# Per-engine order tables, bank holds and expert roundings of a fused attention and mixture-of-experts kernel

## The reference

```python
x = L0_attn_x                       # (16, 512, 128)
xn = _layernorm(x, axis=-1)
x = x + attn(xn) + ffn(xn)

# attn: rmsnorm, 16 heads of 64
h = _rmsnorm(x, norm_scale)
q, k, v = (einsum('bsd,dhe->bshe', h, w) for w in (wq, wk, wv))
weights = softmax(einsum('bqhd,bkhd->bhqk', q * 64 ** -0.5, k))
out = einsum('bqhe,hed->bqd', einsum('bhqk,bkhd->bqhd', weights, v), w_out) + b_out

# ffn: a router (128 -> 512 -> 8) picks two of 8 experts (128 -> 512 -> 128) a token
logits = silu(x @ rw1 + rb1) @ rw2 + rb2
k_logits, k_index = top_k(logits, 2); k_prob = softmax(k_logits)
for e in range(8):
    we = sum(where(k_index == e, k_prob, 0))
    out = out + we[:, None] * (silu(x @ w1[e] + b1[e]) @ w2[e] + b2[e])
```

## Time and profile before

| | |
|---|---|
| median of three runs | 2102.24 us |
| the profiled execution, its own time | 2104.14 us |
| its span (first to last instruction) | 2102.3 us |
| mean granted TensorE clock | 0.987 |
| PE busy | 1966.5 us, 94% |
| DVE busy | 1627.6 us, 77% |
| ACT busy | 1541.4 us, 73% |
| POOL busy | 945.3 us, 45% |

### The profile page before, as it was taken

One profiled execution on the slowest core, in us unless ns is written; L12 is line 12 of the kernel. 1 busy time (PEld: TensorE's weight loads), 2 busy tenths in 40 slices (PEclk: granted clock), 3 DMA queues, 4 the chain that ended last, 5 costly groups with the idle time before them and its releaser, 6 DMA issues.

```text
span 2102.3 us, 45192 instructions
## 1 busy us (share of the span) xinstructions
PE 1966.5 (94%) x16646; PEld 1261.2 (60%) x16646; DVE 1627.6 (77%) x2716; ACT 1541.4 (73%) x3654; POOL 945.3 (45%) x790
## 2 busy tenths in 40 slices
PE   7999999999999999998899999999999999999997
PEld 5655665555656555555566666666665666666654
DVE  6778888887878787777678777777788777777775
ACT  5777877877777777665577777777777777777774
POOL 4334545544343343431035446446455455454454
PEclk9999999999999999999899999999999999999999
DMA  2122322311101111111323334334333333333332
GB/s 82 32 68 88 102 89 95 101 49 41 39 27 38 40 35 42 33 35 44 91 62 79 79 81 83 73 78 80 82 76 77 83 80 83 77 81 78 77 74 46
DMA packets 132697, 141.96 MB, mean 68 GB/s; under 512 B 25438, under 2 KB 99038, under 8 KB 132446
## 3 DMA queue, kind: packets, MB, share of 16 engines
q1 hardware_dynamic: 101886, 118.34, 18.0%
q0 software_dynamic: 30592, 20.73, 8.3%
HBM read 102.65 MB, written 38.46 MB: 67 GB/s over the span
## 4 chain that ended last, share of the span: by engine, by line
PE 65%; ACT 13%; DVE 11%; issue 7%; DMA 1%; another core or an unknown queue 1%; POOL 0%; SPq 0%; DVEq 0%; POOLq 0%; ACTq 0%
PE pair L453 17%; PE pair L394 12%; PE pair L424 9%; PE pair L238 6%; PE pair L240 5%; PE pair L239 4%; ACT PR L409 4%; DVE NM L403 4%; DVE ZZ L772 2%; PE pair L499 2%; PE pair L501 2%; ACT PT L436 2%; ACT ZZ L763 1%; ACT HS L558 1%; DVE PT L439 1%
## 5 line engine op out<-in xcount | busy, mean ns | idle before, releaser
L409 ACT ACTIVATE PR<-pair,NM 128x512 f32<-128x512 f32 x1024 | 712.5, 721 | 55.4 <-DVE NM L403 54.9
L403 DVE TENSOR_REDUCE NM<-pair 128x2 f32<-128x1024 f32 x512 | 610.4, 1211 | 71.8 <-PE pair L394 52.7
L436 ACT COPY PT<-pair 128x512 f32<-128x512 f32 x640 | 360.1, 612 | 362.7 <-PE pair L424 362.5
L394 PE MATMUL pair<-KS,QS 64*128 64x512 f32 x3072 | 492.5, 424 | 35.3 <-DVE KS L379 18.9
L453 PE MATMUL pair<-PT,V 128*64 128x512 f32 x2048 | 470.3, 601 | 5.4 <-ACT PR L409 5.4
L424 PEld LDWEIGHTS pair<-idn,PR 64*128 64x128 f32 x8192 | 337.6, 139 | 130.7 <-ACT HS L558 29.8
L424 PE MATMUL pair<-idn,PR 64*128 64x64 f32 x8192 | 345.9, 223 | 41.9 <-ACT HS L558 18.1
L394 PEld LDWEIGHTS pair<-KS,QS 64*128 64x128 f32 x3072 | 259.7, 187 | 205.3 <-issue 114.3
L778 POOL TENSOR_TENSOR HH<-ZZ,HH 128x512 fp32r<-128x512 f32 x156 | 225.9, 1490 | 325.2 <-DVE HH L777 168.3
L813 POOL DMA_INDIRECT out<-YS,IDW x156 | 244.6, 1568 | 176.1 <-DVE YS L805 118.7
L453 PEld LDWEIGHTS pair<-PT,V 128*64 128x64 f32 x2048 | 136.2, 137 | 268.5 <-issue 248.7
(11 more groups left out here) (168 smaller groups left out, 2905.2 us busy)
## 6 DMA issues: line engine op xcount, KB each, us to landing
E<-w_tab SPq DMA_DIRECT2D x78, 512.0 KB
RB<-l_rows SPq DMA_DIRECT2D x127, 256.0 KB
XG<-slots SPq DMA_DIRECT2D x39, 264.0 KB, 6.4
w_tab<-SPL SPq DMA_DIRECT2D x16, 512.0 KB
l_rows<-RT SPq DMA_DIRECT2D x508, 1.0 KB
xin<-in_x SPq DMA_DIRECT2D x16, 256.0 KB
XQ<-in_x SPq DMA_DIRECT2D x16, 256.0 KB, 6.6
RAW<-in_w SPq DMA_DIRECT2D x16, 256.0 KB
```

Of the source, the lines that this page charges most:

```text
L394: m = e.matmul(bank[bk + j], a[half[j], cols], c[half[j], :], start=(k == 0), stop=(k == 2))
L403: add("dve", lambda e: e.tensor_reduce(NM[:, 2 * t:2 * t + 2], both[:], AX.X, ALU.max, negate=True), needs=[("S", n, t), *([("exp", n - 1, ...
L409: add("act", lambda e: e.activation(PR[:, k, :], bank[bk], ACT.Exp, bias=NM[:, k:k + 1], accum_out=RS[:, n % 2, j, t:t + 1]), needs=[("max ...
L436: add("act", lambda e, r=r: e.copy(dst[r], src[r]), needs=[("T", n, t), *old], name=("PT", n, t, r), place=f"turn{t % 2}")
```

## The change

The tables at the head of the program are set anew, and nothing else is edited.

- `HIGH_ON`: of the four chunks of an expert tile, three are rounded on ACT and one (chunk 1) on DVE; before it was one (chunk 3) on ACT and three on DVE.
- `VALUES_ON`: of the second half of the values, two of four tiles are copied on DVE, not one.
- `PLAN`: `turn` and `in` stand at distance -2, not -3 (and `in` ahead of `turn`), `rows` at -7, not -5. `halves` of chunk 3 keeps distance 1 but goes to `AHEAD`.
- `ACT_ORDER`: in both kinds of group the place `hi` goes behind `side`, and in odd groups `side` goes ahead of `exp11`, the last exponential.
- `DVE_ORDER`: new sequences of places.
- `PE_ORDER`: in odd groups `route` stands ahead of `kq`, not behind `experts`, and `ahead` stands ahead of `T1`. The place `inverse` makes only DVE work.
- `HOLD`: twelve of the seventeen second numbers change, and with them the banks.

```diff
 PE_ORDER = [
-    "S0 T0 S1 T1 inverse kq spread attend ahead weighted experts route".split(),
-    "S0 T0 S1 spread T1 kq ahead attend experts route inverse weighted".split(),
+    "S0 T0 S1 T1 kq spread attend ahead weighted inverse experts route".split(),
+    "S0 T0 S1 ahead spread T1 route kq attend experts weighted inverse".split(),
 ]
 DVE_ORDER = [
-    "inverse max0 turn0 max1 turn1 low values sums side".split(),
-    "max0 turn0 max1 inverse turn1 sums values low side".split(),
+    "inverse max0 max1 turn1 turn0 low values sums side".split(),
+    "sums max0 turn0 max1 turn1 values inverse low side".split(),
 ]
 ACT_ORDER = [
-    "turn0 exp00 exp01 turn1 high exp10 exp11 values hi side".split(),
-    "turn0 exp00 exp01 high values turn1 exp10 exp11 hi side".split(),
+    "turn0 exp00 exp01 high exp10 exp11 values side hi turn1".split(),
+    "turn0 exp00 values exp01 high turn1 exp10 side exp11 hi".split(),
 ]
 TURN_ON = [["act", "act"], ["dve", "act"], ["act", "act"], ["dve", "dve"]]
-VALUES_ON = [["dve", "act", "act", "act"], ["dve", "act", "act", "act"]]
-HIGH_ON = ["dve", "dve", "dve", "act"]
+VALUES_ON = [["dve", "act", "act", "act"], ["dve", "dve", "act", "act"]]
+HIGH_ON = ["act", "dve", "act", "act"]
 PLAN = {
-    -5: [("rows",)],
-    -3: [("turn",), ("in",)],
+    -7: [("rows",)],
+    -2: [("in",), ("turn",)],
     0: [("out",), ("h", 0), ("halves", 0), ("h", 1), ("halves", 1), ("h", 2), ("halves", 2), ("h", 3)],
-    1: [("halves", 3)],
     3: [("y",)],
     5: [("back",), ("add", 0), ("add", 1)],
 }
 AHEAD = {
+    1: [("halves", 3)],
 }
 HOLD = {
-    "S0": (0.9, 4.6), "S1": (0.7, 6.2), "T": (0.5, 2.5), "kq": (0.8, 1.8), "V": (0.8, 2.2), "PV": (3.6, 1.7),
-    "R": (0.2, 2.3), "OP": (1.7, 0.5), "h1": (0.8, 4.3), "w2": (2.9, 1.9), "xg": (0.5, 3.9), "yT": (0.6, 5.1),
-    "r1": (0.8, 3.7), "hT": (0.6, 0.4), "xT": (0.5, 5.2), "oT": (0.5, 2.6), "other": (0.9, 1.3),
+    "S0": (0.9, 5.2), "S1": (0.7, 7.4), "T": (0.5, 3.7), "kq": (0.8, 1.5), "V": (0.8, 1.0), "PV": (3.6, 0.8),
+    "R": (0.2, 1.6), "OP": (1.7, 0.8), "h1": (0.8, 1.9), "w2": (2.9, 1.9), "xg": (0.5, 3.9), "yT": (0.6, 3.3),
+    "r1": (0.8, 3.1), "hT": (0.6, 1.6), "xT": (0.5, 4.6), "oT": (0.5, 1.1), "other": (0.9, 1.6),
 }
```

## The result

The changed kernel takes 2038.62 us (median of four runs, 2036.58 to 2040.24), the kernel before 2102.1 us: ratio 0.9697, 95% interval 0.968 to 0.9713. That is 63.5 us faster.

What follows compares the result with a forecast made beforehand. PE was taken to set the pace, with 49.8 us idle in the expert stage and 44.6 in routing. Terms -25 - 6 - 3 - 2 + 3 + 1 + 1 = -31 us gave 2071 us against the median; range 2048 to 2098 with rivals.

Steps and rivals of the forecast that it cites:

- second rival: PE gains at `YT` but waits next for turned copies at projection and weighted values: 2092 us, chance 0.14.
- small gains: Expert stage: scores on K's low half 6 us, weighted values' banks 3, smaller waits on turned copies 2.
- 5 us of losses: Value copies moved to DVE cost 3 us, the routing stage's new order 1, new bank numbers 1.
- The move of the turn step: Expert stage: gathered rows' step leaves the chunks' group, ending waits on `YT` and `ZZ`: 20 tiles x 1.26, 25 us gained.
- Eight evictions end at 1146.0 + 8 x 0.57 = 1150.6: ACT, sample tile: chunk evictions start near 1146.0 us and run without a wait, 0.57 us each.
- what is late next: After the `YT` wait goes: first copy of turned probabilities, at 1152.6 us; the projection gets its bank at 1153.2, wanted 1153.4.
- Two roundings off DVE: Expert stage, 78 roundings to ACT: earlier maxima and low halves gain 6 us at scores, 3 at weighted values.
- `side` ahead of the last exponential: Odd groups, 19 tiles: exponential ready about 1.4 us after the second product, covered by weighted values; costs nothing, 2.2 us in hand.
- The burst on DVE: Rival: POOL's three low halves together slow a chunk's product on DVE, transposes wait: about 2114 us, chance 0.09.
- PE losing at the next place: Same as the second rival: new PE waits at projection and weighted values, up to 12 us, terms 6 and 3 lost.
- More than I count: Rival: all listed PE waits and the like in the expert stage go, some in routing: 2052 us, chance 0.14.
- The two levels of DVE's rounding: DVE roundings took 426 ns at least, 1377 in the median; the 39 left would fall to the short level; not in the sum.

Runs made afterwards that it cites:

- turn_only: Kernel before with only `turn` and `in` moved from distance -3 to -2 and `halves` of chunk 3 put in `AHEAD`: 2087.91 us, ratio 1.0146.
- high_only: Kernel before with only three of four chunk roundings on ACT and `hi` laid behind `side`: 2054.84 us, ratio 0.9992.
- turn_high: Kernel before with both the moved turn step and three chunk roundings on ACT, all else as before: 2004.49 us, ratio 0.9745.
- x2_two: Kernel before with two buffers for `X2` and nothing moved: 2050.24 us, ratio 0.997.
- hold_only: Kernel before with only the new table `HOLD`, so only the banks change: 2061.62 us, ratio 1.0025.
- after_again: The changed kernel unedited, timed once more against the kernel before on the experiments' chips: 1998.36 us, ratio 0.972.

## Why the forecast had the direction and missed the size

By the distances between the starts of PE's successive blocks, the 58.1 us of the expert stage come from these places (negative is time gained; blocks at the lower clock have a row of their own):

| place | forecast, us | came, us |
|---|---|---|
| transposes and scores behind `YT` and `ZZ`, odd groups behind a chunk group | -25 | -25.2 |
| scores on K's low half | -6 | -11.1 |
| weighted values' banks | -3 | -7.1 |
| transposes in the odd groups with chunks | -2 (with the like) | -7.2 |
| transposes behind `OT`, even groups | 0 | -5.6 |
| projections on `PT` (second rival), odd groups behind and ahead of an even chunk group | 0 | +4.0 and -3.9 |
| transposes behind the moved step's low half | 0 | +5.0 |
| the moved transposes themselves, 0.53 us to the next block, not 0.36 | 0 | +6.5 |
| blocks that ran at the lower clock before | 0 | -6.5 |
| all other blocks | 0 | -7.0 |
| losses by values, order and banks | +5 | none shown |

The forecast's 31 us were 36 us of gains less 5 of losses. Its large term, 25, came at its size, but by luck, as told below. The small gains, 11 us in all, came at 25.4, each above its upper bound (9.7, 5.2 and 5). The 5 us of losses didn't come, the blocks of the lower clock gave 6.5 and the time ahead of the expert stage 4.9; the other places that the forecast had put at nothing cancel within 1 us. These are the second half of the gain. Each entry rests on one trace of each kernel, so small ones may be scatter.

*The move of the turn step, -25.* The waits it names went, and the row has nearly the forecast size, yet as an effect of this edit it was wrong: alone it costs 1.46%. The step that failed is "Eight evictions end at 1146.0 + 8 x 0.57 = 1150.6", taken as the effect of this move alone. In turn_only the seventh of the eight, the fourth `ZT`, waited 2.41 us. ACT runs them through only while DVE returns `ZT`, DVE only while its rounding finds `HH` free, and `HH` is free only behind the second product. The earlier trace rows held the clue: L777's 13.1 us idle, of which 10.3 for L788, small only because the `X2` wait stood before it. The prediction has no term for this idle time: its "what is late next" follows ACT and PE and not DVE between them. Nor has it one for the bank that the moved rows hold one group later, which cost turn_only some 20 us.

*Two roundings off DVE, -6 and -3.* Counted as lighter load. As such it gave nothing (high_only, 0.9992). Within the whole change it is worth 2.9 points (1.0014 against 0.972), about 60 us, since it takes the remaining rounding behind two products of chunks. The terms were added up as if each acted by itself; the two edits open two gates in series (the buffers of `X2` and of `HH`), and only both together let much through. That the first row of the table fits its forecast is luck: it does so only because the other edit, forecast as a small one, opened the second gate.

*The ceiling.* The prediction says of the change that "all it can give or cost is idle time of PE", 49.8 us in the expert stage. That was false: 58.1 came there, and only 40.4 us of idle time went. The small terms were bounded in the same way, by PE's waits in the earlier trace rows and by what they leave of 49.8 us, and so was the rival that set the lower end of the range. A sure ceiling wants the starts of PE's blocks, not the busy time.

*`side` ahead of the last exponential, 0.* Held: weighted values have no row among PE's waits after.

*The rivals.* The burst on DVE did not come: the longest product of a chunk fell from 5.50 us to 2.32, and 5 of 156 products ran beside a low half of POOL, at 0.90 to 2.32 us. In tile 4 the fourth product ran at 1145.04 us and POOL began its first low half at 1146.95, once it had issued the four row adds (L813) ahead of it; the forecast had no row for these. PE losing at the next place came at 4.7 us, not 21. "More than I count", 2052, was nearest, and even it was held down by the ceiling. In the routing stage PE's idle time is 38.0 us (44.6 before), a little outside the 5 us given.

*The two levels of DVE's rounding.* The 39 roundings left on DVE fell to 427 ns in the median, as the forecast said. By the rule of the Trainium skill (SBUF — State Buffer, "SBUF: two separate sides"), VectorE in a two-port mode and GpSimd lock a shared port pair, and the loser blocks for the whole instruction. The trace agrees with it: before, the 64 roundings beside a tensor operation of POOL took 1386 ns in the mean and the other 53 took 435, and after, none of the 39 ran beside one. For the time it mattered little where a rounding is fast: it takes 0.43 us on DVE and 0.70 on ACT after, yet three on ACT give 0.9745 (turn_high) where three on DVE, even with the second buffer, give 0.9819.

## What to carry to other kernels

Where an in-order engine waits for a single-buffered tile, look for the next single-buffered tile in the same chain before you price the first: a wait of 10 us behind one of 59 us may be a second gate, which takes the whole wait over when the first is opened. Price two such edits together, and test a pair of buffers early, since it takes a wait away without moving an instruction, while a moved step brings waits of its own. Read PE's ceiling from block starts, and count a wait that is left as harmless only where what is queued behind it has slack.

## What the runs showed of the hardware

- The same DVE rounding of 128x512 took 435 ns in the mean where no tensor operation of POOL ran beside it (53 of the 117 before) and 1386 ns where one did (64). After, the 39 took 427 ns in the median. On ACT the same rounding took 636 ns in the mean before and 702 after.
- In the expert stage before, from 1591.8 to 1595.1 us, the granted clock was 0.50, and successive 128x512 products on PE started 0.43 us apart; at the full clock they start 0.23 us apart (1137.76 to 1138.00 after).
- The kernel before took 2102 us where it was first measured and 2055.4 to 2056.3 on the four chips of the experiments. turn_only, x2_two and hold_only have its code of the routing stage, but for hold_only's banks: their groups 8 to 128 took 830.6 us, against 870.9 in the first profile. The changed kernel had 867.2 there and 833.5 in after_again. The two profiles of the first measurement have DVE waits in this stage whose releaser the profile gives only as `remote` (before: 13.7 us ahead of maxima and 11.8 ahead of turned copies; after: 14.9 and 4.4) and PE waits for `PT` of 13.9 and 12.1 us; turn_only has neither. What causes them wasn't found. The ratio of the changed kernel hardly depends on it: 0.9697 there, 0.972 here.
